# Graph 3 of g moved ahead of the second chunk of v, with four neighbouring orders changed

## What is computed

```python
H  = (adj != 0);  w = adj[:, 0, :]
conv(x, W, b) = Dn * (H @ (Be * (H.T @ (x @ W.T)))) + b     # Dn = 1/(H @ w), Be = 1/column sums of H
h  = layer_norm(relu(conv(x, W1, b1))) * gamma + beta        # 256 -> 512 features
y  = conv(h, W2, b2)                                         # 512 -> 256 features
out = layer_norm(x + (y + x))
```

## Time and profile before

| | |
|---|---|
| median of 3 launches | 289.74 us (289.73 to 290.66) |
| the profiled execution | 290.7 us |
| its span, first to last instruction | 288.9 us |
| TensorE matmul busy | 277.7 us, 96% |
| VectorE busy | 227.9 us, 79% |
| ScalarE busy | 195.6 us, 68% |
| GpSimd busy | 138.6 us, 48% |
| mean granted TensorE clock | 0.996 of full speed |

### The profile page before, as it was taken

How to read it: one execution, slowest core, us unless ns; L and a number is a source line. 1 busy time by engine, 2 the same in 40 slices (tenths; PEclk the granted TensorE clock), 3 DMA queues, 4 the chain that set the end, 5 groups by cost and what they waited for, 6 DMA issues and landing times.

```text
span 288.9 us, 5778 instructions
## 1 busy us (share of the span) xinstructions
PE 277.7 (96%) x1814; PEld 249.0 (86%) x1814; DVE 227.9 (79%) x660; ACT 195.6 (68%) x556; POOL 138.6 (48%) x193
## 2 busy tenths in 40 slices
PE   6899999999999999999999999999999999999991
PEld 6779979898898989899898989899898989889880
DVE  1676579787979888797978888797988879596884
ACT  3288977766767876676677877676678775583614
POOL 2224463637364563636374463636365364536362
PEclk9999999999999999999999999999999999999998
DMA  7920140433513434431433533333423322120104
GB/s 218 309 79 19 40 127 16 112 113 63 173 41 122 113 94 115 122 114 54 152 70 93 140 99 109 100 104 53 136 50 91 97 88 75 36 73 2 50 25 145
DMA packets 37255, 27.70 MB, mean 96 GB/s; under 512 B 10013, under 2 KB 35305, under 8 KB 37225
## 3 DMA queue, kind: packets, MB, share of 16 engines
q1 hardware_dynamic: 37120, 27.30, 33.3%
q10 hardware_dynamic: 104, 0.04, 0.1%
HBM read 17.21 MB, written 8.42 MB: 89 GB/s over the span
## 4 chain that ended last, share of the span: by engine, by line
PE 85%; DVE 7%; issue 2%; POOL 2%; DMA 2%; ACT 1%; DVEq 0%; SPq 0%; POOLq 0%
PE bank_v L291 29%; PE bank_g L308 10%; PE bank_g L301 10%; PE bank_g L303 10%; PE bank_v L325 9%; PE bank_v L276 9%; PE bank_s L255 5%; PE bank_g L318 2%; DMA w_raw<-in_L_gnn_W_dram 2%; POOL rstd L870 1%; DVE g_sb L652 1%; DVE r_lo L661 1%; DVE pair_sb L666 1%; PE bank_g L333 1%; PE bank_g L353 1%
## 5 line engine op out<-in xcount | busy, mean ns | idle before, releaser
L886 POOL TENSOR_TENSOR xb_sb<-x_sb,b_half 128x512 f32<-128x512 f32 (+1 forms) x31 | 41.2, 1331 | 75.6 <-DVE r_lo L661 51.6
L481 ACT ACTIVATE r_sb<-bank_v,vec 128x512 f32<-128x512 f32 x64 | 44.2, 691 | 36.4 <-PE bank_v L291 35.7
L301 PE MATMUL bank_g<-w_hi,r_hi 128*128 128x258 f32 x256 | 65.5, 288 | 0.0
L303 PE MATMUL bank_g<-w_lo,r_hi 128*128 128x256 f32 x256 | 63.8, 282 | 0.0
L894 POOL TENSOR_SCALAR r_hi<-r_sb 128x512 fp32r<-128x512 f32 x64 | 47.9, 749 | 32.4 <-ACT r_sb L481 32.3
L661 DVE TENSOR_TENSOR r_lo<-r_sb,r_hi 128x512 fp32r<-128x512 f32 x64 | 44.7, 719 | 11.1 <-POOL r_hi L894 11.1
L291 PE MATMUL bank_v<-u_hi,w_hi 128*128 128x512 f32 x128 | 50.7, 396 | 0.4 <-DVE u_lo L625 0.4
L291 PE MATMUL bank_v<-u_hi,w_lo 128*128 128x512 f32 x128 | 50.8, 397 | 0.0
L291 PE MATMUL bank_v<-u_lo,w_hi 128*128 128x512 f32 x128 | 50.6, 395 | 0.0
L301 PEld LDWEIGHTS bank_g<-w_hi,r_hi 128*128 128x128 f32 x256 | 48.3, 189 | 1.4
L303 PEld LDWEIGHTS bank_g<-w_lo,r_hi 128*128 128x128 f32 x256 | 48.1, 188 | 1.2
(11 more groups left out here) (99 smaller groups left out, 449.1 us busy)
## 6 DMA issues: line engine op xcount, KB each, us to landing
x_sb<-in_x_dram SPq DMA_DIRECT2D x16, 512.0 KB, 3.8
out_dram<-z_sb SPq DMA_DIRECT2D x15, 512.0 KB, 3.2
adj_sb<-in_adj_dram SPq DMA_DIRECT2D x16, 256.0 KB, 4.0
d_row<-d_rows SPq DMA_DIRECT2D x13, 256.0 KB, 3.4
w_raw<-in_L_gnn_W_dram SPq DMA_DIRECT2D x2, 512.0 KB, 5.9
out_dram<-z_sb SPq DMA_DIRECT2D x2, 256.0 KB, 2.6
turned_h<-h_sb SPq DMA_TRANSPOSE x13, 2.4
d_rows<-dinv SPq DMA_DIRECT2D x13, 2.0 KB, 2.1
```

The lines of the kernel that those rows point to most:

```text
L301: pe.matmul(bank_g[:, n, 0:W2COLS], r_hi[:, i % 2, k, graph(n)], w2_hi[:, k], start=(k == 0), stop=False)
L303: pe.matmul(bank_g[:, n, 0:DOUT], r_hi[:, i % 2, k, graph(n)], w2_lo[:, k], start=False, stop=False, skip_group_check=True)
L481: nc.scalar.activation(r_sb[:, k], bank_v[:, k % 2], ACT.Relu, bias=vec[:, k:k + 1]).then_inc(relu_ready, 1)
L886: nc.gpsimd.tensor_tensor(xb_sb[:, i % 2, part], x_sb[:, i % 3, part], b2_half[:, :].unsqueeze(1).to_broadcast([P, n, DOUT]), ALU.add).the ...
```

## The change

Five orders change, and no instruction is added, removed or altered. On TensorE, in steps 1 to 14, graph 3 of g comes before chunk 1 of v, so that chunks 1, 2 and 3 of v follow one another. (Step 0 keeps its order; only its text is merged.) On ScalarE, in steps 1 to 14, the first half of `normalise(i - 1)` comes before relu and square of chunk 1 and not after them. On VectorE, the first hidden variance comes ahead of the output statistics, and `read_g(i, 0)` ahead of `make_var2(i - 1)`. On GpSimd, the second half of `add_b2` comes behind the first hidden power; r_hi of chunk 0 comes ahead of `inverse_std2`, and the second hidden power ahead of r_hi of chunk 1.

```diff
@@ TensorE
                     make_s(2)
-                elif i < LAST:
-                    make_v(i + 1, 1)
                 make_g(i, 3)
                 if i == LAST:
                     break
-                if i == 0:
-                    make_v(1, 1)
+                make_v(i + 1, 1)
                 make_v(i + 1, 2)
                 make_v(i + 1, 3)
@@ ScalarE
                     square(i + 1, 0)
+                if i:
+                    normalise(i - 1, 0)
                 relu(i + 1, 1)
                 square(i + 1, 1)
-                if i:
-                    normalise(i - 1, 0)
                 relu(i + 1, 2)
@@ VectorE
                     make_b(i + 3)
+                make_var1(i, 0)
+                if i:
                     take_stats2(i - 1, 0)
                     take_stats2(i - 1, 1)
-                make_var1(i, 0)
+                read_g(i, 0)
                 if i:
                     make_var2(i - 1)
-                read_g(i, 0)
                 if i + 4 < G:
                     make_h(i + 4)
                 split_r(i + 1, 0)
@@ GpSimd
-                for half in range(2):
-                    add_b2(i, half)
+                add_b2(i, 0)
                 inverse_std1(i, 0)
+                add_b2(i, 1)
+                split_r(i + 1, 0)
                 if i:
                     inverse_std2(i - 1)
-                split_r(i + 1, 0)
+                inverse_std1(i, 1)
                 split_r(i + 1, 1)
-                inverse_std1(i, 1)
                 split_r(i + 1, 2)
```

## The result

| | before | after |
|---|---|---|
| median | 289.74 us (289.73 to 290.66, 4 runs) | 292.66 us (292.57 to 292.70, 4 runs) |
| ratio, with its 95% interval | | 1.0093 [1.0073, 1.0112] |
| span of the profiled execution | 288.9 us | 290.8 us |
| TensorE busy | 277.7 us | 277.6 us |

What follows compares the result with a forecast made beforehand. TensorE, busy 96% of the span, was taken as the bound. 1.4 + 0.9 + 0.6 + 0 = 2.9 us on the 289.74 median gave 292.6 us; range 289.5 to 296.0, the forecast case's own 291.0 to 294.0.

Steps and rivals of the forecast that it cites:

- The wait of y1: On TensorE, y1 waits 0.24 us per step for relu of chunk 3; the change keeps this wait.
- relu 1 behind normalise behind shift2: On ScalarE, relu 1 follows normalise, which waits for GpSimd's shift2; relu 1 starts 0.36 us behind the end of v1.
- Where TensorE waits: TensorE loses time at y1, 1.23 us and not 1.10, about 1.57 in steps 12 and 13; v3 isn't late.
- rival 1: Nothing comes late enough: shift2 ends by 135.6, only step 0 costs, about 289.9 us; chance 0.33.
- The two meetings on the ports: VectorE and GpSimd delay each other: negated mean meets r_hi of chunk 0, +0.05 us; inverse_std2 meets make_h, +0.12.
- The rival of the full lock: Shared ports lock for whole instructions: inverse_std2 loses 0.26 us, y1 0.27 per step in 1 to 11, 294.2; chance 0.10.
- Price per step, 1 to 11: y1 on TensorE pays 0.13 us in each of steps 1 to 11, 1.4 us in all.
- ScalarE's free pace: ScalarE takes 1.28 us from relu to relu when free, against v's 1.39, so relu 1 may start 0.23 late.
- Steps 12 and 13: Without make_h, r_lo of chunk 0 takes the ports ahead of inverse_std2: 0.47 us in each step, 0.9 in all.
- Step 0: GpSimd's new order delays r_hi of chunk 0 and the chain to y1: 0.6 us, ends 0.3 and 0.9.
- The end: From step 14 on, q could come 0.55 us earlier but relu 3 is late: 0, ends -0.55 and +0.3.
- rival 3: r_lo of chunk 0 gets the ports ahead of inverse_std2 in all steps, y1 0.76 us late, 299.6; chance 0.06.

Runs made afterwards that it cites:

- e7: Kernel before, with s of group i + 3 cut in two around y1 in steps 1 to 12: 288.00 us, ratio 0.9941.
- e3: Changed kernel with both halves of normalise behind the square of chunk 3: 290.48 us, ratio 1.0020.
- e2: Kernel before with only the TensorE order changed (g3 ahead of chunk 1 of v): 300.17 us, ratio 1.0348.
- e9: Changed kernel with make_var2(i - 1) ahead of read_g(i, 0) on VectorE again, as before: 290.58 us, ratio 1.0024.
- e5: Changed kernel with make_h(i + 4) moved behind r_lo of chunk 0 on VectorE: 296.25 us, ratio 1.0236.
- e6: Changed kernel with r_lo of chunk 0 behind the second variance in steps 12 to 14 alone: 291.58 us, ratio 1.0070.
- e4: Changed kernel with GpSimd's old order in step 0 alone: 291.57 us, ratio 1.0052.
- e1: Kernel before run again without any edit, for a second trace: 289.72 us, ratio 0.9993.

## Why the prediction was right, step by step

The number came out, and so did the chain up to relu 3. The place of TensorE's loss was wrong in part, and one sign of the text's own list failed.

- **The wait of y1** for relu of chunk 3, which the change keeps: held, and e7 shows that it is real time (y1 0.86 with s in between).
- **relu 1 behind normalise behind shift2:** held. The text had relu 1 0.36 later than v1 alone would allow; it is 0.40 (v2 starts at 136.65; in e3, where relu 1 waits for v1 only, it starts 0.20 behind v2; here it starts at 137.25). In step 12 it is 0.72, where the text had 0.70. e2, e3 and e9 each move one link and get the time that the chain gives, e9 by a smaller step than expected.
- **Where TensorE waits:** missed in part. The text had v3 in time, y1 at 1.23, and at about 1.57 in steps 12 and 13, and said that it is wrong if y1 stays at 1.10. y1 stays at 1.10 (1.12 in step 13). Half of the loss in steps 1 to 11 and 0.35 of the 0.40 in steps 12 to 14 stand in v3, which waits for relu 1. The text compared the end of relu 1, plus 0.14, with the end of v2 in the chain. But the first matmul of the next piece starts 0.17 before that end (y0 at 138.97 in TensorE's order of time before, v3's end at 139.14), so by the text's own terms v3 had nothing to spare and not 0.17. In step 6 relu 1 ends at 137.92, 0.13 before v3's first matmul (138.05), and the second matmul comes 0.04 late; in step 12 it ends at 237.24, when that matmul is already due (237.05). The sum barely suffers, since a late v3 takes up time in which y1 would have waited for relu 3; but whoever went by y1 alone would have taken rival 1 for true. Rival 1's own sign, shift2's end, tells it rightly: by the start of the hidden variance (131.19 here, 130.71 there) it comes at 135.74 on the axis of step 6, behind the 135.6 that rival 1 needs.
- **The two meetings on the ports:** held. Taken were +0.05 for the mean and +0.12 for inverse_std2; measured 0.08 (0.25 against 0.17) and 0.11 (1.12 against 1.01). The rival of the full lock, 0.26, falls: the earlier trace rows were the better guide than the letter of the Trainium skill ("SBUF — State Buffer", "Who interferes with whom"), where the blocked engine waits for the whole instruction. That GpSimd waits for VectorE, and that the order of asking decides whether it does, as the section says, e5 and e6 show. The reverse does not hold for this instruction: the text let r_lo wait when inverse_std2 asks first, but r_lo started 0.17 into it and took 0.68, as when alone.
- **Price per step, 1 to 11:** taken 0.13, measured 0.085, so 0.9 and not 1.4. The mis-sized term is ScalarE's free pace: 1.28 came from step 0; it is 1.24 here, relu taking 0.67 and not 0.69 or 0.70. So ScalarE has 0.31 to spare and not 0.23, and 0.40 - 0.31 = 0.09.
- **Steps 12 and 13:** taken 0.47 each, measured 0.40 (0.72 - 0.31 = 0.41), and the reason shown by e5 and e6: r_lo asks first. The wait is v3's and not y1's.
- **Step 0:** taken 0.6; measured 1.07 (e4: 1.0), above its range of 0.3 to 0.9. The place was right. The second read_g starts at 39.93, 0.60 later than in e1 and not 0.42: r_hi of chunk 0 met make_h, and they took 0.80 and 0.64 (0.62 and 0.42 in e1). Behind it come r_lo at 40.72, the pair at 41.46 (1.09 beside r_hi, 0.68 in e1) and z at 42.48, for which u waits: the other 0.41. That pile-up was named and priced too low.
- **The end:** taken 0, with relu 3 late in step 14. The period 13-14 lost 0.40, and 0.22 came back behind y0 of step 14: +0.18.
- **Rival 1** (nothing late) and **rival 3** (r_lo first everywhere) were not idle: e9 makes the like of the former, at 290.58, and e5 of the latter, at 296.25. Rival 3's 299.6 let make_h and r_lo both go ahead; in e5 only r_lo does.

The sum was nearer than its terms, and that is luck: they were too high by 0.5 in steps 1 to 11 and 0.1 in 12 and 13, too low by 0.5 in step 0 and 0.2 at the end. That the 2.9 could be added to the median also held, for a reason that the text didn't know (e1: a late start in one profiled execution).

## What to carry to other kernels

When one engine is busy 96% of the time, an order is judged by the engine that must keep its pace: count that engine's free pace against the leader's (here 1.24 against 1.39), and each instruction with a foreign wait that is put ahead of it must fit in the difference. When VectorE and GpSimd share a critical chain, look at which instruction asks for the ports just before the other's: exchanging two neighbours was worth 3.6 us. A wait that recurs in every step, however small (0.24), is filled best by independent work that is at hand.

## What the runs showed of the hardware

- The same GpSimd instruction on 128x4 took 1.02 us with VectorE idle for its first 0.63 (e6), 1.12 when it started 0.17 into a VectorE instruction of 0.42 with one SBUF source, and 1.43 when it started 0.14 into one of 0.69 with two (e5). In both it lost what was left of VectorE's, less about 0.14 (0.25 left and 0.11 lost; 0.55 and 0.42).
- It did not hold VectorE up: r_lo, with two SBUF sources, started 0.17 into it in the changed kernel and took 0.68. r_hi did: the sum of squares that started 0.02 into r_hi's 0.62 took 1.13 and not 0.68, so it lost what was left of r_hi (0.60), less 0.15.
- relu of chunks 1 to 3, back to back with the squares, took 0.67 each in step 6 of the changed kernel, and 0.69 or 0.70 in step 0 of the kernel before. Why is open.
- One kernel's start differs by 0.94 us between two executions (y0 of step 0 at 40.11 and 39.17). In the later one the transposes of W1 waited until the load of W1 had landed at 6.00.
